# A fixed first key block with the range search moved into it, and two weight pieces per product in half of an expert mixing

## The reference

```
_lenS2 = 4096 - randint(0, 1025)
mask   = logical_not(arange(4096) < _lenS2)      # (256, 4096), all rows alike
out    = softmax(q k^T / 8 where mask, else -inf) v
```

```
hidden = gelu(x down^T)                           # (256, 4096)
weight = sum over picks of relu(score) one_hot(expert)   # (256, 4096)
y      = (hidden * weight) up
```

## Time and profile before

| | |
|---|---|
| median of 3 runs | 447.14 us |
| the profiled execution, and its span | 448.73 us, 446.9 us |
| TensorE busy (products) | 423.9 us, 95% |
| weight loads, overlapping them | 305.4 us, 68% |
| VectorE busy | 263.5 us, 59% |
| ScalarE busy | 168.8 us, 38% |
| granted TensorE clock, mean | 0.996 |

### The profile page before, as it was taken

How to read it: one execution, slowest core, us unless ns; L and a number is a source line. 1 busy time by engine, 2 the same in 40 slices (tenths; PEclk the granted TensorE clock), 3 DMA queues, 4 the chain that set the end, 5 groups by cost and what they waited for, 6 DMA issues and landing times.

```text
span 446.9 us, 8130 instructions
## 1 busy us (share of the span) xinstructions
PE 423.9 (95%) x3087; PEld 305.4 (68%) x3087; DVE 263.5 (59%) x892; ACT 168.8 (38%) x429; POOL 2.5 (1%) x10
## 2 busy tenths in 40 slices
PE   6989999999999999788999999999999998989997
PEld 5645554554555789666768799988757767877774
DVE  6255554776768657787499899231436554464433
ACT  3265556656666217774413310000333323242110
POOL 1000000000000000000000000000000000000000
PEclk9999999999999999999999999999999999998999
DMA  8500010000029184000199300049292000000000
GB/s 282 171 1 1 1 47 1 1 2 1 0 80 350 51 277 194 1 1 1 41 352 324 103 3 3 1 157 220 68 394 65 0 1 0 1 2 0 0 1 24
DMA packets 24518, 36.07 MB, mean 81 GB/s; under 512 B 1694, under 2 KB 20768, under 8 KB 23968
## 3 DMA queue, kind: packets, MB, share of 16 engines
q1 hardware_dynamic: 24192, 35.48, 24.6%
q10 hardware_dynamic: 288, 0.07, 0.1%
HBM read 35.29 MB, written 0.26 MB: 80 GB/s over the span
## 4 chain that ended last, share of the span: by engine, by line
PE 46%; issue 41%; DVE 10%; ACT 1%; DMA 1%; POOL 0%; POOLq 0%; DVEq 0%; SPq 0%
PE bank L925 6%; PE bank L1149 6%; PE bank L916 6%; PE bank L1019 5%; PE bank L994 3%; PE bank L999 2%; PE bank L1163 2%; PE bank L1008 2%; DVE region_a L1774 2%; PE bank L890 1%; PE bank L1167 1%; DVE region_a L1771 1%; PE bank L771 1%; PE bank L706 1%; PE bank L970 1%
## 5 line engine op out<-in xcount | busy, mean ns | idle before, releaser
L1224 ACT ACTIVATE region_g<-bank,nm_new 128x384 f32<-128x384 f32 (+1 forms) x64 | 40.1, 633 | 32.4 <-DVE nm_new L1530 20.0
L1522 DVE CUSTOM_DVE_ANT_0 bank<-bank,bias_h 128x384 f32<-128x384 f32 (+1 forms) x64 | 38.7, 646 | 11.3 <-issue 11.2
L585 PEld LDWEIGHTS bank<-ident,region_g 128*128 128x128 f32 x226 | 24.1, 141 | 22.8 <-issue 9.0
L585 PE MATMUL bank<-ident,region_g 128*128 128x128 f32 x226 | 32.2, 281 | 1.9 <-ACT region_g L1224 1.2
L622 PE MATMUL bank<-region_a,qT 64*128 64x384 f32 (+1 forms) x128 | 32.6, 567 | 0.5 <-ACT region_g L1224 0.3
L925 PE MATMUL bank<-region_u,region_g 128*128 128x256 f32 x128 | 29.3, 383 | 0.0
L605 PE MATMUL bank<-region_d,region_a 128*64 128x256 f32 x232 | 28.6, 386 | 0.0
L890 PE MATMUL bank<-xnT,region_d 128*128 128x256 f32 x128 | 28.0, 379 | 0.0
L1210 ACT COPY region_d<-bank 128x512 f32<-128x512 f32 (+1 forms) x48 | 24.2, 538 | 9.9 <-PE bank L585 9.9
L1149 PE MATMUL bank<-xnT,region_u 128*128 128x256 f32 (+1 forms) x112 | 27.2, 402 | 0.0
L890 PEld LDWEIGHTS bank<-xnT,region_d 128*128 128x128 f32 x128 | 24.2, 190 | 3.7 <-issue 0.5
(11 more groups left out here) (354 smaller groups left out, 758.8 us busy)
## 6 DMA issues: line engine op xcount, KB each, us to landing
region_d<-in_downT SPq DMA_DIRECT2D x2, 2048.0 KB, 11.0
region_u<-in_up SPq DMA_DIRECT2D x2, 2048.0 KB, 11.6
region_a<-in_ctx SPq DMA_DIRECT2D x1, 3072.0 KB, 15.9
region_d<-in_ctxT SPq DMA_DIRECT2D x1, 2048.0 KB, 9.7
region_d<-in_ctxT SPq DMA_DIRECT2D x2, 1024.0 KB, 16.0
region_u<-in_wg SPq DMA_DIRECT2D x1, 1728.0 KB, 7.4
region_u<-in_wu SPq DMA_DIRECT2D x1, 1728.0 KB, 11.8
region_a<-in_wd SPq DMA_DIRECT2D x1, 1664.0 KB, 15.4
```

Of the source, the lines that this page charges most:

```text
L585: mm = nc.tensor.transpose(bank[4 + e][:, k * P:(k + 1) * P], prob[:, u % 2, e, k * P:(k + 1) * P], ident[:, :])
L1224: nc.scalar.activation(prob[:, u % 2, e, 0:tiles * P], bank[2 * s + e][:, 0:tiles * P], ACT.Exp, scale=-1.0, bias=nm_new[:, p, t, e:e + 1] ...
L1522: ins = nc.vector.tensor_tensor_reduce(bank[2 * s + e][:, 0:size], bank[2 * s + e][:, 0:size], bias_h[:, t, 0:size], -1.0, 3e38, ALU.add, ...
```

## The change

The first block of 384 keys is always the last 384 keys of the context (`TAIL` = 3712). The range now covers only what lies before it, and the search runs among the pairs of the first block: block search on VectorE after pairs 0 and 1, the count on TensorE in pair 3 (`COUNT_AT`), `find_range` ahead of pair 4, the token marks ahead of pair 5. The DMAs, the start of TensorE's list and the register loads move with it. In the mixing, the second token half takes two of the three score pieces in one product of 64 columns and adds the third to the first; ScalarE copies the second piece out of PSUM, VectorE adds it and multiplies. Core of the diff:

```diff
 # SyncE
-            (x, mask in two, Wq in two, block ends, Wkv first half, wait for the range,
-             384 keys at the range's begin, Wkv second half, pick_pair, rows)
+            load_block(TAIL, FIRST)                       # right behind x
+            load_wkv(0, wkv_in)
+            (Wq in two)
+            for t, (lo, hi) in enumerate(((TAIL // 4, S2 // 4), (0, TAIL // 4))):
+                sp.dma_start(mask_w[:, :, lo:hi], mask words lo to hi, both token halves).then_inc(mask_in[t], 16)
+            load_wkv(1, wkv_rest_and_pick_in)
+            (block ends, pick_pair, rows)
+            sp.wait_ge(range_set, 1)
             first = sp.value_load(rng_i[0:1, 0:1], min_val=0, max_val=GROUPS - 1)
...
-            load_block(within(first * GRP + FIRST * P, S2 - GRP + FIRST * P), KT_PER)
+            load_block(within(first * GRP, S2 - BLK), KT_PER)
...
-            sp.wait_ge(mixw_psum, 4 * HALF)
+            sp.wait_ge(mixw_psum, 6 * HALF)
 # TensorE
+            for k in range(SPARE):                        # 15, as before; the 8 later ones are gone
+                nc.tensor.transpose(bank[7][:, k % 4 * P:(k % 4 + 1) * P], ident[:, :], ident[:, :])
+            turn_xn(pe, 1, (bank[6], bank[7]))
             pe.wait_ge(ctx_landed, 16)
+            pe.wait_ge(wkv_in, 48)
             keys_and_values(0, FIRST)
-            pe.wait_ge(q_ready, 4)
             keys_and_values(1, FIRST)
+            pe.wait_ge(wq_in[0], 16)
+            pe.wait_ge(xnT_ready, 2)
+            queries((0, 1))
+            pe.wait_ge(wq_in[1], 16)
+            queries((2, 3))
+            pe.wait_ge(q_ready, 1)
             for p in range(XP):
                 scores(p, 0, FIRST, 0, 0)
+                if p == 0:
+                    queries((4, 5, 6, 7))
+                if p == 1:
+                    pe.wait_ge(q_ready, 4)
+                if p == COUNT_AT:
+                    pe.wait_ge(blocks_seen, 1)
+                    (the two counting products, into bank 7)
...
                 scores(p, 1, FIRST, 0, 0)
+                if p == 0:
+                    pe.wait_ge(q_ready, 2)
                 turn(p, 0, FIRST, 0, 0)
...
             pe.wait_ge(pads_set, 4)
+            pe.wait_ge(range_set, 1)
+            n_turns = pe.value_load(rng_i[0:1, 1:2], min_val=1, max_val=NTURN)
             with pe.Fori(0, n_turns) as i:
...
+            def mix_weights_in_two(n):
+                pe.wait_ge(hot_ready, n + 1)
+                for g in (2 * n - HALF, 2 * n - HALF + 1):
+                    pe.wait_ge(hidden_ready, g - 2)
+                    for j in range(MS):                   # 8 tokens
+                        s = g % 2 * MS + j
+                        for w, pieces in ((0, slice(0, 2)), (1, slice(2, 3))):
+                            for k in range(2):
+                                own = slice(64 * k, 64 * k + 64)
+                                into = bank[MIXED[g % 3] + k][:, :].rearrange("p (w h s) -> p w h s", w=2, h=ET)
+                                mm = nc.tensor.matmul(into[:, 0:2 - w, :, j], lhsT=hot_lo[n % 3][own, :, s],
+                                                      rhs=hot_hi[n % 3][own, pieces, :, s], start=w == 0, stop=w == 1)
+                                if j == MS - 1 and w == 1:
+                                    mm.then_inc(mixw_psum, 1)
-            for n in range(HALF + 1):
+            for n in range(HALF):
                 mix_weights(n)
+            mix_weights_in_two(HALF)
...
                 if n < 2 * HALF:
-                    mix_weights(n)
-            pe.wait_ge(hidden_ready, 2 * HALF)
+                    mix_weights_in_two(n)
+            pe.wait_ge(hidden_ready, 3 * HALF)
 # ScalarE
             copy_keys(0, FIRST, 0)
             copy_keys(1, FIRST, 0)
+            for j in range(3):
+                copy_queries(j)
...
                     exps(p, 0, FIRST, 0, 0, sums)
+                if p == 0:
+                    copy_queries(3)
                 exps(p, 1, FIRST, 0, 0, sums)
...
+            act.wait_ge(range_set, 1)
+            n_turns = act.value_load(rng_i[0:1, 1:2], min_val=1, max_val=NTURN)
             with act.Fori(0, n_turns) as i:
...
+            for g in range(HALF, 3 * HALF):
+                act.wait_ge(mixw_psum, 2 * g + 2)
+                if g >= HALF + 2:
+                    act.wait_ge(hidden_ready, g - 1)
+                parts = banks[:, MIXED[g % 3]:MIXED[g % 3] + 2, :].rearrange("p k (w h s) -> p k w h s", w=2, h=ET)
+                nc.scalar.copy(weight_sum[g % 2], parts[:, :, 1]).then_inc(last_piece_copied, 1)
 # VectorE
-            find_blocks()
-            find_range()
-            (the three operations for is_row, two value_loads)
-            set_bias(within(first * GRP, S2 - GRP), FIRST, 1)
             copy_values(0, FIRST, 0)
             copy_values(1, FIRST, 0)
+            dve.wait_ge(mask_in[0], 16)
+            set_bias(TAIL, FIRST, 1)
             for p in range(XP):
+                if p == COUNT_AT + 1:
+                    find_range()
+                if p == COUNT_AT + 2:
+                    (the three operations for is_row)
                 maxima(p, 0, FIRST, 0, nm_new).then_inc(nm_ready, 1)
...
                 if p + 2 < XP:
                     copy_values(p + 2, FIRST, 0)
+                if p < TT:
+                    find_blocks(p)      # one token half; after the second also the clip to 1 and
+                                        # mask_w[:, :, TAIL // 4:S2 // 4] = 0
             dve.wait_ge(nm_ready, 2 * XP)
             keep_maxima(1)
+            dve.wait_ge(range_set, 1)
+            (the two value_loads)
...
+            def weigh_in_two(n):
+                for g in (2 * n - HALF, 2 * n - HALF + 1):
+                    dve.wait_ge(mixw_psum, 2 * g + 2)
+                    dve.wait_ge(last_piece_copied, g - HALF + 1)
+                    b, at = MIXED[g % 3], (n - HALF) * GS + g % 2 * MS
+                    own = hidden_sh[:, 1, :, :, at:at + MS]
+                    parts = banks[:, b:b + 2, :].rearrange("p k (w h s) -> p k w h s", w=2, h=ET)
+                    step(nc.vector.tensor_tensor(weight_sum[g % 2], parts[:, :, 0], weight_sum[g % 2], ALU.add))
+                    nc.vector.tensor_tensor(own, weight_sum[g % 2], own, ALU.mult).then_inc(hidden_ready, 1)
 # the table of block ends: ends clipped to GROUPS - BEGUN = 58, turns asked for every 8 groups from 0
```

More of the change, by code:

```diff
@@ L31 @@
 BEGUN = FIRST * P // GRP
+SPARE = 15
+COUNT_AT = 3
 NTURN = (GROUPS - BEGUN + PER - 1) // PER
+TAIL = S2 - FIRST * P
 PAD = 1024
@@ L41 @@
 GS = 16
+MS = GS // 2
 HALF = P // GS // 2
@@ L182, in build @@
         rest_w = part(region_a, 7744, P)
+        weight_sum = [part(region_a, at, 512).rearrange("p (k h s) -> p k h s", k=2, h=ET) for at in (4864, 5632)]
         iota = part(region_a, 5120, P)
@@ L571, in keys_and_values, with queries @@
                 mm.then_inc(kv_psum, 1)
-            pe.wait_ge(wkv_in, 48)
-            pe.wait_ge(blocks_counted, 1)
-            pe.wait_ge(range_set, 1)
-            n_turns = pe.value_load(rng_i[0:1, 1:2], min_val=1, max_val=NTURN)
+            def queries(tiles):
+                for m in tiles:
+                    dst = bank[4 + m // 2][:, (m % 2) * T:(m % 2 + 1) * T]
+                    for c in range(DC):
+                        mm = nc.tensor.matmul(dst, lhsT=wq[:, c, m * P:(m + 1) * P], rhs=xnT[:, c, :],
+                                              start=c == 0, stop=c == DC - 1)
+                    if m % 2:
+                        mm.then_inc(q_psum, 1)
             def turn(p, t, tiles, base16, base32):
@@ L637, in _ @@
                 scores(p, 0, FIRST, 0, 0)
+                if p == 0:
[4 more added lines that the diff above has]
+                    pe.wait_ge(blocks_seen, 1)
+                    for t in range(TT):
+                        mm = nc.tensor.matmul(bank[7][0:1, T:T + GROUPS], lhsT=ones[:, 0:1], rhs=seen[:, t, :],
+                                              start=t == 0, stop=t == TT - 1)
+                    mm.then_inc(blocks_counted, 1)
                 if p == XP - 1:
@@ L685, in _ @@
             values(-1, KT_PER, end8, end16)
-            pe.wait_ge(pick_in, 16)
             pe.wait_ge(lT_ready, 1)
@@ L1196, in _, with copy_queries @@
             for c in range(DC):
-                nc.scalar.activation(xnT[:, c, :], bank[c][:, 0:T], ACT.Identity, bias=column("L0_xattn_ln_beta", c),
+                nc.scalar.activation(xnT[:, c, :], bank[6 + c][:, 0:T], ACT.Identity, bias=column("L0_xattn_ln_beta", c),
                                      scale=column("L0_xattn_ln_gamma", c)).then_inc(xnT_ready, 1)
-            for j in range(4):
+            def copy_queries(j):
                 act.wait_ge(q_psum, j + 1)
@@ L2117, in laid_out @@
                                for j in range(2)], axis=1).astype(np.float32).reshape(P, -1),
[L2118 to L2119 removed]
```

(2 more changed lines are left out.)

101 lines of the change are left out of this document (37 added, 64 removed).

## The result

The changed kernel took 450.24 us (median of 22 executions), the kernel before 449.4 us over as many beside it: the ratio is 1.0046, with a 95% interval of 1.0028 to 1.0063. By this ratio it is 0.5% slower (the two medians are 0.84 us apart), where 0.6% faster was forecast, and 450.24 us lies above the range of 442.0 to 448.0. The interval excludes 1, but the difference is inside the 1% that the prediction called no change. The profiled execution took 450.92 us with a span of 449.1 us, 2.2 us more than the span of 446.9 us before.

A forecast was written before the change was run, and what follows sets the result against it. TensorE, busy 95% of the span, was taken as the bound. Mixing's gain of 3.5 us less a first-block net loss of 0.95 saves 2.55 us, from 447.14 to 444.6 us; range 442.0 to 448.0.

The forecast's parts named there:

- Start of the first block, gain 2.2: Head of the kernel: keys and values 0 and 1 ahead of queries bring keys and values 2 to 23.3 from 25.49.
- the landing at 7.8: Head of the kernel: the first Wkv set lands at 7.8 us, between ends of 7.49 and 10.7.
- the late-landing rival: Head of the kernel: first weights land at 10.7, costing 2.9 us more, 447.5 us in all; chance 0.05.
- the first pair at 2.77 us: Head of the kernel, TensorE: each of the first two key and value steps takes 2.77 us, together 5.5.
- Search, loss 3.15: First block's pairs: losses of 1.2 in pair 1, 0.4 for counting, 0.8 in pair 4, 0.75 at the register load.
- the way into the loop: Between first block and loop: the register load of the turn count lies bare, loss 0.75 us (0 to 0.8).
- Flags and second block search: VectorE in the first block's pairs: row flags and second search fit idle time or slack and cost nothing.
- Mixing, gain 3.5: Mixing, second token half: groups of 2.44 us instead of 3.33, saving 3.5 us (0.8 to 4.2).
- the price of a float32 query column: Mixing: upper bound of 0.88 ns a column, 28 ns per wide product; half of it, 14 ns, was taken.
- The rival of dear wide products: Mixing: wide products pay the float32 column price, gain only 0.8 us, 447.3 us in all; chance 0.08.
- The argument by overlapping halves: Mixing: products in alternating row halves overlap, as score products do, so 14 ns is charged once per token.
- The new work on VectorE and ScalarE: Mixing: PSUM copies fall in ScalarE's idle time; VectorE's 1.35 us per half group stays ahead of TensorE's needs.

The follow-up runs named there:

- placed: The changed kernel with VectorE's search steps moved behind the score work of their pair, out of the way of the maxima; 448.61 us (one run).
- b_only: The kernel before with only the new mixing of the second token half; 448.62 us, ratio 0.9996.
- wkv_first: The changed kernel with SyncE issuing Wq, mask and the rest only once the first Wkv set has landed; 448.38 us, ratio 0.9996.
- moving_close: The changed kernel, timing only, with the mixing products' moving operand read from adjacent elements instead of every 16th; 2.09 us a group, 448.66 us.
- narrow_close: The kernel before, timing only, with its 96 narrow mixing products reading moving elements side by side; 3.09 us a group, 450.14 us.
- best_mix: The kernel before with the new mixing reading side by side and VectorE writing one-hots scattered into that layout; 467.85 us, ratio 1.041.
- all_mended: The changed kernel with side-by-side mixing reads, scattered one-hot writes, 14 identity products, Wq and mask held back, and search moved behind score work; 465.83 us, ratio 1.0376.
- two_steps: The changed kernel with start and search mended and one-hots laid out in token pairs, so TensorE steps by 4 bytes; 442.32 us, ratio 0.9853.
- warm: The changed kernel with 20 more identity transposes between the turned tokens and the first keys; 449.44 us, ratio 1.0023.
- a_only: The changed kernel with the mixing of before, leaving only the first block's part; 450.2 us, ratio 1.0028.

## Why the prediction was wrong

By its own steps:

- **Start of the first block, gain 2.2: wrong by 5.15 us**, and this alone turns the sign. Its first half, the landing at 7.8, took the bytes that the first 7 us had moved before (236 GB/s) as if the new order would move them as fast and one after the other; 188 GB/s were moved, and Wkv, with Wq and mask issued behind it, landed at 10.6 (about 2.8 us more, and near the 10.7 of the late-landing rival, which had a chance of 0.05). Its second half priced the first pair at 2.77 us because that was its row, but that row stood behind 6 us of queries. Behind 2.70 us of idle time it took 5.27 (2.5 us more), at the lower clock. The rival had the place right and the price by half: it would give 447.5.
- **Search, loss 3.15: right**, 3.03 measured. Piece by piece, by the table of steps: pair 1 1.02 (forecast 1.2), counting 0.32 (0.4), pair 4 0.75 (0.8; its wait of 0.45 is only part of it), the way into the loop 0.95 (0.75; the gap alone is 0.78). Flags and second block search cost nothing that shows, as forecast: pairs 2 and 5 take what they took before. The reason given, that only work ahead of maxima counts, is shown by placed.
- **Mixing, gain 3.5: mis-sized.** Measured 0.13 or so a group and 0.5 to 0.7 in all. The step that failed is "the 32 more columns at most cost the price of a float32 query column", 28 ns, and that half of it is enough; a wide product costs 30 ns more than a narrow one, because of the step, and the two row halves do not hide it: charged once per product, 16 x 2 x 30 ns are the 0.96 us that turn 2.23 into 3.20. The rival of dear wide products (0.8 us of gain) was the right one; it had 0.08. The argument by overlapping halves held for score products, whose moving columns are side by side.
- **The new work on VectorE and ScalarE: hidden**, as forecast.
- Not foreseen: the 1.3 us at the index table and the 1.7 us in the mixture of experts, in favour of the change. Without them the profiled execution would be about 5.2 us (1.2%) longer than before.

Sum by the measured terms: -2.95 (start) - 3.03 (search) = -5.98 at the loop, +0.7, +1.3, +1.7 = -2.3 us.

Part of the distance between 444.6 and 450.24 is not of the change at all: the forecast started from a median of three executions, 447.14, and over 22 the kernel before has 449.4. With that start the forecast of 2.55 us saved would have read 446.9, still with the wrong sign.

Open: why the index table lands 1.7 to 1.9 us after its issue in every kernel with the new start and 3.2 to 3.4 us in those with the old one; and where the stretch of low granted clock falls. Before, b_only, wkv_first, moving_close, narrow_close, best_mix, all_mended and two_steps have 8.7 to 8.8 us for those 32 products, the others 7.15; warm has a slow stretch ahead of them, at 385 to 388 us. It is not a property of a kernel alone: the 79 executions of the kernel before that stand beside four of the runs took about 447.4 us at a mean granted clock of 0.998 to 1.0, 448.9 at 0.994 to 0.996 and 450.3 at 0.991 or 0.992. No run was made to tell what decides it. A difference of 1.7 us between two single executions can be of this kind, so the 1.7 us above explain the two profiled executions and not the ratio.

## What to carry to other kernels

Before merging products, divide their time by their columns: if it is about 1 ns a column at a wide step, as here, the read is the price, and merging saves nothing until the layout changes; then cost the engine that writes that layout, too. Before moving work to the head of a kernel, ask what the engine did in the microseconds before it, and take its duration from a row with the same neighbour. Work that is slipped in goes behind what feeds the next engine in line, not ahead of it.

## What the runs showed of the hardware

- The first 128x384 and 128x512 pairs of products took 1.62 and 1.90 us in a_only, after 3.07 us of idle time and at a granted clock of 0.50, and 0.88 and 1.02 us in warm, after identity products. In the changed kernel they took 1.62 and 1.91 us, though the row reads 1.00:

```profile
10.50:15.80 5.30, 5.21 (x8) 1.67 (x8) 0.00 (x0) 0.00 (x0) 0.00 (x0) 1.00 1.05 362
```

  The Trainium skill, page "TensorE: Matmul & The Clock Gate", section "What's actually happening", says that an array that has been idle runs at 1.2 GHz instead of 2.4. The durations agree (ratios of 1.84 and 1.87), and so does a_only's 0.50.
- 1536 bf16 elements on VectorE: 0.95 us in order, 1.09 in three instructions with runs of two, 1.75 with one operand repeated innermost, 2.9 with another read 32 bytes apart besides, 7.8 written 192 bytes apart.
- Weights that lie side by side saved 0.26 us per 64 products (2.94 against 3.20) even while the moving operand was read at its 32-byte step.
